# Scores three units ahead, row maxima sent per batch, one bank for the output projections: a change to an attention and expert kernel

## The reference

```
x = x + xattn(layernorm(x), ctx, ctx)     # 16 heads of 16, softmax over 128 context tokens
x = x + ffn(layernorm(x))                 # top-1 of 8 experts, 256 -> 64 (exact gelu) -> 256
scores = einsum('bthd,bshd->bhts', wq, wk) / sqrt(16)
attn   = einsum('bhts,bshd->bthd', softmax(scores), wv);  y = attn @ wo.T + bo
```

## Time and profile before

| what | value |
|---|---|
| runs, median of 3 | 1676.08 |
| the profiled execution's own time | 1676.87 |
| its span in the profile | 1674.8 |
| TensorE busy (matmul) | 1532.9, 92% |
| VectorE busy | 1226.1, 73% |
| ScalarE busy | 925.6, 55% |
| GpSimd busy | 425.9, 25% |
| chain that ended last, by engine | PE 72%, DVE 17%, issue 5%, ACT 5%, DMA 1% |

### The profile page before, as it was taken

One profiled execution on the slowest core, in us unless ns is written; L12 is line 12 of the kernel. 1 busy time (PEld: TensorE's weight loads), 2 busy tenths in 40 slices (PEclk: granted clock), 3 DMA queues, 4 the chain that ended last, 5 costly groups with the idle time before them and its releaser, 6 DMA issues.

```text
span 1674.8 us, 40310 instructions
## 1 busy us (share of the span) xinstructions
PE 1532.9 (92%) x15566; PEld 1225.3 (73%) x15566; DVE 1226.1 (73%) x2878; ACT 925.6 (55%) x1578; POOL 425.9 (25%) x599
## 2 busy tenths in 40 slices
PE   6599999999999999999999999967999999999998
PEld 4477777777777777777777777855777777777776
DVE  4777777777777777777777777755777777777775
ACT  3276667667766776667666766643333423333342
POOL 3122222222322232232222222212223232322321
PEclk8699999999999999999999999997999999999999
DMA  4454456445644554555455545511121212212121
GB/s 120 109 156 137 127 147 165 135 128 148 166 133 132 151 163 128 140 151 156 128 149 151 155 125 148 138 56 45 57 76 51 76 57 71 72 55 76 51 76 38
DMA packets 148385, 190.36 MB, mean 114 GB/s; under 512 B 15531, under 2 KB 99046, under 8 KB 148198
## 3 DMA queue, kind: packets, MB, share of 16 engines
q1 hardware_dynamic: 148198, 187.79, 40.3%
HBM read 52.48 MB, written 33.55 MB: 51 GB/s over the span
## 4 chain that ended last, share of the span: by engine, by line
PE 72%; DVE 17%; issue 5%; ACT 5%; DMA 1%; SPq 0%; POOL 0%; ACTq 0%; DVEq 0%
PE s_ps L495 12%; PE st_ps L513 11%; PE pp_ps L1148 8%; DVE negmax L893 7%; PE pv_ps L1094 6%; PE s_ps L1051 6%; PE pp_ps L1156 5%; PE pp_ps L1121 4%; PE st_ps L1079 3%; PE pv_ps L1102 3%; PE t_ps L1070 2%; PE pp_ps L461 2%; PE s_ps L502 2%; PE t_ps L1062 2%; PE pp_ps L1142 2%
## 5 line engine op out<-in xcount | busy, mean ns | idle before, releaser
L893 DVE TENSOR_REDUCE negmax<-s_ps 128x8 f32<-128x1024 f32 x256 | 313.3, 1224 | 144.7 <-PE s_ps L1051 137.4
L788 ACT ACTIVATE pT<-st_ps 128x1024 f32<-128x1024 f32 x256 | 263.1, 1028 | 99.8 <-PE st_ps L1079 99.2
L513 PE MATMUL st_ps<-w_hi,q_packed 128*128 128x256 f32 x1024 | 213.5, 293 | 0.7 <-DVE q_packed L415 0.7
L701 POOL TENSOR_TENSOR q_parts<-q,q_parts 128x1024 bf16<-128x1024 f32 x32 | 68.3, 2134 | 537.5 <-ACT q_parts L782 537.5
L1094 PE MATMUL pv_ps<-pT,v 128*32 128x128 f32 x4096 | 166.4, 278 | 27.7 <-DVE attn L909 18.9
L495 PE MATMUL s_ps<-k_packed,w_hi 128*128 128x512 f32 x512 | 173.9, 421 | 18.0 <-ACT pT L324 18.0
L513 PEld LDWEIGHTS st_ps<-w_hi,q_packed 128*128 128x128 f32 x1024 | 168.0, 188 | 10.5 <-issue 6.4
L318 ACT ACTIVATE offhotT<-pv_ps 96x512 bf16<-96x512 bf16 x32 | 19.0, 593 | 257.5 <-PE pv_ps L482 257.5
L1079 PE MATMUL st_ps<-q_packed,k_packed 98*128 98x128 bf16 x2048 | 157.9, 220 | 3.4 <-DMA q_packed<-negmaxT 2.0
L1051 PE MATMUL s_ps<-k_packed,q_packed 96*128 96x128 bf16 x2048 | 158.4, 220 | 2.0 <-DVE negmax L893 1.3
L1051 PEld LDWEIGHTS s_ps<-k_packed,q_packed 96*128 96x128 bf16 x2048 | 128.2, 98 | 24.6 <-issue 20.9
(11 more groups left out here) (164 smaller groups left out, 3646.5 us busy)
## 6 DMA issues: line engine op xcount, KB each, us to landing
q_packed<-q_parts SPq DMA_DIRECT2D x192, 256.0 KB, 3.8
k_packed<-k_parts SPq DMA_DIRECT2D x192, 256.0 KB, 4.2
xin<-in_x_dram SPq DMA_DIRECT2D x32, 512.0 KB, 3.7
cin<-in_ctx_dram SPq DMA_DIRECT2D x32, 512.0 KB, 3.6
x_scratch<-xb SPq DMA_DIRECT2D x32, 512.0 KB, 5.2
xin<-x_scratch SPq DMA_DIRECT2D x32, 512.0 KB, 4.7
out_dram<-xb SPq DMA_DIRECT2D x32, 512.0 KB, 3.2
q_packed<-negmaxT SPq DMA_DIRECT2D x256, 4.0 KB
```

What stands on the lines that cost most here:

```text
L513: t.matmul(o, h[n % 2][:, m, tok].bitcast(F32R), w[:, m, :].bitcast(F32R), start=(m == 0 and k == 0), stop=False)
L701: g.tensor_tensor(parts[z][:, 2, :, :], z32[z][:], parts[z][:, 1, :, :], ALU.subtract).then_inc(s_lo, 1)
L788: a.activation(pT[u % 2][:], st_ps[:], ACT.Exp, scale=DH ** -0.5).then_inc(s_exp, 1)
L893: v.tensor_reduce(negmax[u % 2][:], s_ps[:].rearrange("p (h s) -> p h s", s=P), AX_X, ALU.max, negate=True).then_inc(s_red, 1)
```

## The change

Scores run three units ahead instead of two, so `negmax` has four buffers. The maxima of a batch's two units are gathered in one 128x32 tile, turned once, copied once and sent once, in even units: per group four turnings, four copies and four transfers of 8 KB take the place of eight of 4 KB. Item k of a group moves one unit later or earlier as `SLICES` says, with the steps on ScalarE, VectorE and SyncE that follow from it: `mid` and `normalise` come one unit earlier, the statistics of rows 2 and 3 are both taken in u1. All output projections use bank 1. In u4 the values of the unit before come ahead of the projection; in u5 item 3 comes behind the values.

```diff
-        negmax = [sb(f"negmax{n}", [P, HC]) for n in range(2)]
-        negmax_p = [sb(f"negmax_p{n}", [P, 2 * HC], BF16) for n in range(2)]
-        negmaxT = [sb(f"negmaxT{n}", [2 * HC, P], BF16) for n in range(2)]
+        negmax = [sb(f"negmax{n}", [P, HC]) for n in range(4)]
+        negmax_p = [sb(f"negmax_p{n}", [P, 2, HC, C], BF16) for n in range(2)]
+        negmaxT = [sb(f"negmaxT{n}", [2 * H, P], BF16) for n in range(2)]
-        Y_BANK = (0, 1, 0, 0)
+        y_ps = pp_ps[1][:, 0:D]
-        SLICES = [((1, 5),), ((1, 6),), ((1, 7),), ((1, 8),), ((1, 9),), ((2, 0), (2, 1)), ((2, 2), (2, 3)), ((2, 4),)]
+        SLICES = [((1, 6),), ((1, 7),), ((1, 8),), ((1, 9),), ((2, 0),), ((2, 1), (2, 2), (2, 3)), ((2, 4),), ((2, 5),)]
# SyncE, group(g), the order after:
+                if g + 2 <= LAST:
+                    load_c(g + 2)
+                if g < LAST:
+                    pack(g + 1, 0, 0)
+                load_max(g, 1)
+                if g < LAST:
+                    pack(g + 1, 0, 1)
+                    pack(g + 1, 0, 2)
+                    pack(g + 1, 1, 0)
+                load_max(g, 2)
+                if g < LAST:
+                    pack(g + 1, 1, 1)
+                if g > 0:
+                    store_x2(g - 1)
+                if g < LAST:
+                    pack(g + 1, 1, 2)
+                load_max(g, 3)
+                if g + 3 <= LAST:
+                    load_x(g + 3)
+                if g < LAST:
+                    load_max(g + 1, 0)
# ScalarE, group(n), after exp(n, u):
-                    if more and u == 1:
+                    if more and u == 0:
                         mid(n + 1, 0)
-                    if more and u == 3:
+                    if more and u == 2:
                         mid(n + 1, 1)
-                    if more2 and u == 4:
+                    if more2 and u == 3:
                         normalise(n + 2)
+                    for ahead, k in SLICES[u]:
+                        if n + ahead <= LAST:
+                            item(n + ahead, k)
+                    if nxt and u % 2 == 0:
+                        keep_max(nxt[0], nxt[1] // 2)
# VectorE, group(n):
-                    if more and u < 4:
-                        remainder(n + 1, 4 + u)
-                    if later(n, u, 2):
-                        maxima(*later(n, u, 2))
+                    if more and u < 3:
+                        remainder(n + 1, 5 + u)
+                    if more2 and u == 6:
+                        lower(n + 2, 3)
+                    if more2 and u == 7:
+                        remainder(n + 2, 4)
+                    if later(n, u, 3):
+                        maxima(*later(n, u, 3))
+                    rows_due = [(n + 2, 1)] if u == 0 else [(n + 2, 2), (n + 2, 3)] if u == 1 else [(n + 3, 0)] if u == 7 else []
...
+                    if more2 and u == 4:
+                        lower(n + 2, 0)
                     if more2 and u == 5:
-                        lower(n + 2, 0)
                         lower(n + 2, 1)
-                    if more2 and u == 6:
                         lower(n + 2, 2)
-                    if more2 and u == 7:
-                        lower(n + 2, 3)
# TensorE, the order of a unit after:
             def even(n, u):
+                ahead, nxt, done, before = later(n, u, 3), later(n, u, 2), turned_at(n, u), later(n, u, -1)
+                if ahead:
+                    scores(*ahead)
                 scoresT(n, u)
                 items(n, u, slice(0, 1))
+                if u == 4:
                     values(*before)
                 if done:
                     project_out(*done)
                 if nxt:
+                    turn_max(nxt[0], nxt[1] // 2)
+                if u != 4 and before[0] >= 0:
                     values(*before)
             def odd(n, u):
+                    scores(*ahead)
                 scoresT(n, u)
                 if done:
                     turn_pv(*done)
                 items(n, u, slice(0, 2))
-                if nxt:
-                    turn_max(*nxt)
                 values(n, u - 1)
+                items(n, u, slice(2, 3))
                 if done:
                     turn_attn(*done, nxt)
```

More of the change, by code:

```diff
@@ L614, in _ @@
             load_x(2)
-            for u in range(2):
-                load_max(0, u)
+            load_max(0, 0)
             def group(g):
@@ L735, in _, with keep_max @@
             a = nc.scalar
[L737 to L741, removed]
+            def keep_max(n, b):
+                act.wait_ge(s_mt, at(PAIRS, n, b + 1))
+                wait(act, ld_mx[b % 2], 16 * at(PAIRS // 2, n, b // 2))
+                a.copy(negmaxT[b % 2][:], maxT_ps).then_inc(s_mte, 1)
             def keep_pvT(n, b):
@@ L809, in _ @@
             mid(0, 1)
-            for k in range(5):
+            for k in range(6):
                 item(1, k)
             act.wait_ge(s_set, SETUP_DVE)
-            for u in range(2):
-                keep_max(0, u)
+            keep_max(0, 0)
             def group(n):
@@ L985, in _ @@
                 lower(1, k)
-            for u in range(2):
+            remainder(1, 4)
+            for u in range(3):
                 maxima(0, u)
@@ L1136, in item @@
                     pe.wait_ge(s_r, at(4, n, k - 5))
[L1138 to L1139 removed]
+                if k in (1, 5, 7, 9):
+                    wait(pe, s_x2, at(GB, n - 2, {1: 1, 5: 2, 7: 3, 9: 4}[k]))
                 if k < 4:
@@ L1214, in _ @@
             pe.wait_ge(s_pad, 2)
-            for u in range(2):
+            for u in range(3):
                 scores(0, u)
-            for u in range(2):
-                turn_max(0, u)
+            turn_max(0, 0)
             def even(n, u):
-                nxt, done, before = later(n, u, 2), turned_at(n, u), later(n, u, -1)
-                if nxt:
-                    scores(*nxt)
+                ahead, nxt, done, before = later(n, u, 3), later(n, u, 2), turned_at(n, u), later(n, u, -1)
+                if ahead:
+                    scores(*ahead)
                 scoresT(n, u)
                 items(n, u, slice(0, 1))
-                if u == 6:
+                if u == 4:
                     values(*before)
@@ L1230, in even @@
                 if nxt:
-                    turn_max(*nxt)
-                if u != 6 and before[0] >= 0:
+                    turn_max(nxt[0], nxt[1] // 2)
+                if u != 4 and before[0] >= 0:
                     values(*before)
-                items(n, u, slice(1, 2))
             def odd(n, u):
-                nxt, done = later(n, u, 2), turned_at(n, u)
-                if nxt:
-                    scores(*nxt)
+                ahead, nxt, done = later(n, u, 3), later(n, u, 1), turned_at(n, u)
+                if ahead:
+                    scores(*ahead)
                 scoresT(n, u)
```

105 lines of the change are left out of this document (30 added, 75 removed).

## The result

The changed kernel took 1660.45 us, the median of four runs (1654.17 to 1662.47), against 1676.77 for the kernel before: a ratio of 0.9895, 95% interval 0.9867 to 0.9923. The forecast was 1663.5. The profiled execution is the shortest one, 1654.17.

What follows compares the result with a forecast made beforehand. The prediction took VectorE's chain to bound odd units, and that chain or TensorE's work even ones. Unit terms summed to -0.42 per group, -12.6 over some 30 groups: 1664.3 from the profiled 1676.9, forecast 1663.5, range 1645 to 1690.

Steps and rivals of the forecast that it cites:

- VectorE's chain sets the odd units, and TensorE's work or that chain the even ones: Attention units: VectorE's dependent steps set odd units' length; even units follow a chain too, but TensorE's work bounds u4.
- u1, +0.29 for the second statistics step: In u1, two statistics steps ahead of the division instead of one: +0.29, bounds 0 and 0.42, giving 4.49.
- u4, -0.07, from a store landing at 4.8 and keys at S + 7.5: u4 ends when the last keys land behind the store; S is u3's start; u4 3.69, -0.07.
- The rival of late keys: At u5's start, scores of the next group's u0 wait for late keys: slower, 1680 to 1711; chance 0.22.
- my 3.16: Length of u4 if nothing waits for the keys, the lower bound.
- u5, -0.05, with 0.2 left of GpSimd's part: u5: 4.35 by chain and item 3, plus 0.2 where GpSimd's residual delays hi: 4.55 against 4.6, -0.05.
- the rival of a GpSimd still in the way: In u5 GpSimd's residual covers hi and lo: 5.01, sum +0.04 a group, 1677; chance 0.13 for 1673 to 1682.
- its point of decision: The GpSimd rival in u5 needs the store to land 0.5 or more later without the keys doing so.
- Its other form: GpSimd's lo parts end only 0.4 ahead of u3's hi part; a slip of 0.4 could cost up to 2 us a group.
- u6 and u7, -0.08 and -0.03: u6: a bank wait goes, but lower of item 3 precedes the reduction, 4.19, -0.08; u7: 4.20, -0.03.
- Four turnings, copies and transfers fewer: 0: Per group, fewer turnings lie beside VectorE's division and transfer waits lie off the chain: 0; transfer bounds 0 and -0.28.
- The sum: All units' terms together: -0.42 per group, some 30 groups, -12.6 us.

Runs made afterwards that it cites:

- e4: The changed kernel with the statistics steps behind the division and behind the lo part of the attention result, instead of ahead of them; 1632.11 us, ratio 0.9732.
- e7: The kernel before with the statistics steps behind the division and the lo part of the attention result; 1651.03 us, ratio 0.9854.
- e2: The changed kernel with one wait added, so that GpSimd's residual runs beside the hi and lo parts of u5; 1678.3 us, ratio 1.0018.
- e3: The changed kernel with the last transfer of the keys issued ahead of the store instead of behind it; 1667.57 us, ratio 0.9953.
- e5: The changed kernel with each unit's maxima turned, copied and sent by themselves again, scores still three ahead; 1721.94 us, ratio 1.0274.
- e9: The changed kernel with each unit's maxima by themselves, but turned and copied early in odd units; 1664.09 us, ratio 0.9937.
- e1: The kernel before with one wait added: GpSimd's residual starts only after the lo part of the group's last maxima; 1667.84 us, ratio 0.9951.
- e8: The changed kernel run again without any edit, beside other experiments; 1665.06 us, ratio 0.9926 to the kernel before.

## Why the prediction was right

*VectorE's chain sets the odd units, and TensorE's work or that chain the even ones.* Right: u0, u1, u2 and u3 came out within 0.03, with no rows of the changed kernel seen. e4 shows the chain itself by shortening it, and e7 shows a limit of the rule: in u7 of the kernel before, TensorE's work was as long as the chain.

*u1, +0.29 for the second statistics step.* Right in kind, 0.33 in size.

*u4, -0.07, from a store landing at 4.8 and keys at S + 7.5.* Mechanism right, size off: -0.22, as stores landed 4.2 after their issue in the median, and the good group's keys landed 6.9 after the start of u3. The rival of late keys happened in single groups, up to 1.5 over the floor at once, and not in the mean. That floor, u4 without a wait, is 3.27 and not my 3.16.

*u5, -0.05, with 0.2 left of GpSimd's part.* Same term again: -0.30, since the earlier store also put the residual wholly ahead of hi and lo. 4.36 is the 4.35 of the chain. e2 and e3 show the rival of a GpSimd still in the way as a real price, 0.6 in each, and that its point of decision was near: in e3 the store was issued 0.7 later in its unit and the price was there in every group. Its other form did not happen: GpSimd's lo part of the keys ended 0.44 ahead of the hi part of u3 in the group shown, and u3 stayed at 3.91 or 3.92 in all groups.

*u6 and u7, -0.08 and -0.03.* Neither came. In u6 the reduction started 1.21 into the unit, not 1.16, and in u7 4.20 should have been 4.24: 0.1 a group lost on readings of a few hundredths each.

*Four turnings, copies and transfers fewer: 0.* Right as a price, wrong as a whole thought. I named VectorE's division as the cover on TensorE and did not ask what would stand ahead of ScalarE's copy if it stayed: e5 puts 2.3 a group on that in u3 and u5. The section of the Trainium skill that I cited (DMA: Bandwidth & Descriptors, Anatomy of one DMA) gives its 2.0 us for transfers that GpSimd issues. Those here are issued by SyncE, and by e9 128 of them fewer were worth 8 us at most. The order of the new schedule would not have worked without the pairs, or without e9's other place for the copy.

*The sum.* -12.6 forecast; 16.3 by the medians of the first runs, 11.8 in the second set. Per group, the two mis-sized terms of u4 and u5 give 0.40 more than forecast, and u1, u6, u7, u0 and u2 take 0.19 of it back. That the sum came within 4 us of both medians is thus in part luck: errors of opposite sign, and medians that gained 5 to 6 us less than the profiled executions did.

## What to carry to other kernels

Write down the length of each stage of a repeating schedule and what it is made of; then a reordering can be costed in tenths of a microsecond, and the mean of one varying stage points to a transfer or a lock. On an engine in order, what stands ahead of the step that another engine waits for is the cost, not what the engine does in all: moving four statistics steps a group behind that step gave more than the whole change. When two transfers with deadlines share a queue, look at what each landing releases (here GpSimd's work as well as TensorE's) before either is moved.

## What the runs showed of the hardware

A VectorE operation with two SBUF inputs waited for GpSimd's running one to end, in whole parts: 0.64 instead of 0.17 for lo in e2, and 0.167 in the mean of 233 when e1 kept GpSimd away. The Trainium skill (SBUF — State Buffer, SBUF: two separate sides) has the shared pair of ports as an exclusive lock for the whole instruction; by that rule the trace agrees. VectorE's division and `lower`, with one operand in PSUM, ran beside the residual at their usual lengths, 0.42 (e2) and 0.69 (the changed kernel).

The landing of one and the same transfer, the last keys, was 4.4 after its issue in one group and 5.9 in another of the same execution, with the same transfers ahead. A schedule that needs it within 4.6 pays in some groups only. How much of the spread between executions comes from this is open. In e3, where u4 is 3.26 or 3.27 throughout, ten of twelve executions lie within 2.4 us, and the two that are 6 and 9 us longer have the lowest mean granted clocks, 0.972 and 0.975. But e4, whose u4 goes from 3.26 to 5.09, has its four within 1.8.

A late landing can cost twice. In e8 one u4 lasted 4.60; the scores behind it, and the 4 us after (columns as in the earlier trace rows):

```profile
879.20 0.86 PE L1022 MATMUL s_ps<-k_packed,q_packed 96*128 96x128 bf16 x8 [1.27 <-issue]
```

```profile
880.00:884.00 4.00, 3.79 (x37) 3.36 (x35) 2.97 (x7) 2.20 (x3) 0.00 (x0) 0.65 0.43 131
```

TensorE had stood idle for 1.27, and the granted clock fell for a while from 1.00 (2.4 GHz) towards the lower level (1.2 GHz): u5 lasted 5.60 instead of 4.35. Three groups of e4 show the same. It did not follow every time: the changed kernel's first profile has u4 of 4.66 and 4.78 and no such fall.

TensorE's granted clock in the stretch where the attention stage ends differs between executions. In windows of 1100 to 1200 us (columns as in the earlier trace rows), first the changed kernel, then e9, whose profiled execution was the longest of its seven, 1678.27, while their median was 1664.09:

```profile
1100.00:1200.00 100.00, 86.92 (x618) 65.42 (x619) 64.79 (x186) 35.80 (x57) 25.47 (x47) 0.93 0.20 64
```

```profile
1100.00:1200.00 100.00, 85.50 (x636) 64.47 (x628) 54.73 (x155) 33.05 (x54) 19.31 (x37) 0.76 0.15 49
```

The means of 0.93 and 0.76 lie between the levels of 2.4 and 1.2 GHz. The kernels differ little, and the changed kernel itself, run again as e8, had 0.88 there. In its first profile TensorE was busy 5.9 to 7.4 of every 10 us from 1070 to 1110 and the clock, 0.94 in the last of them, was 0.67 from 1110 to 1120; in e9's it was busy 9.62 from 1070 to 1080, and the clock was 0.67 in the 10 us after. What makes the difference was not found.
